# A message-passing kernel: how messages are added into their destination nodes, and how TensorE gets its addresses

## The chip, the cores and the metric

The kernel runs on one core of one Trainium2 chip. The metric is the device time of one execution in microseconds (us). The engines are PE (TensorE; PEld is its weight loads), DVE (VectorE), ACT (ScalarE), POOL (GpSimd) and SP (which here only issues transfers). Each has an in-order sequencer that decodes its instructions, computes registers and loads them, and hands the work to the engine proper; rows of a sequencer carry a q behind the engine's name (PEldq, POOLq).

## The reference

A graph of 3125 nodes with 64 features and 100,000 edges, sorted by destination. First three rounds with the same weights:

```python
msg_in = concat([h[src], h[dst], edge_attr], axis=1)
msg = silu(msg_in @ W1e + b1e) @ W2e + b2e
agg = segment_sum(msg, dst) / max(deg, 1)
h = h + silu(concat([h, agg]) @ W1n + b1n) @ W2n + b2n
```

After a residual and a layer norm, three relational layers: per relation the mean of `h[src]` over the edges of that relation into a node, times that relation's weight, plus a root term. A residual and a norm end it. All data is float32.

## The kernel before

Nodes stand in 25 blocks of 128 (`NB`), sources in 13 spans of two blocks (`NS`). A setup stage (to about 1522 us) ranks the edges and scatters their records (edge term, source place, destination place, type) into tiles of 128 edges whose sources lie in one span and whose destinations in one block. Eight tiles (`GT`) are a group, all with one destination block; there are `NG` = 160 groups. Then come six loops over the 160 groups: `l` = 0 to 2 are the rounds of the first network ("round 0" to "round 2" below), `l` = 3 to 5 the relational layers.

In a round, one group `g` runs through this:

- TensorE gathers. `gather_tile` (L871, L872, L875) multiplies three transposed one-hots of the tile (`ohT`: source in the span's first block, in its second, destination) by a table of node terms split in three bf16 parts, 192 columns wide. The table's column comes from registers, since the span and the block differ from tile to tile and from group to group. 24 matmuls fill four PSUM banks (`gat`); a half is two banks, and DVE must have read the half (`gat_read`) before the next group writes it.
- DVE adds the three parts and the record's edge term into `z`: three tensor_tensor for each half (L1274, L1277, L1280).
- ACT takes Silu into `msg` (L655), in float32.
- The scatter needs a one-hot of the destination places, `oh`, in float32. POOL compares four tiles of it (L523); ACT makes the other four with an Abs (L648) and a Relu (L652).
- TensorE, two groups later, adds `oh` times `msg` into PSUM (L897): 8 float32 matmuls of 64 columns (68 in round 0, which counts types), at a PSUM column from a register. PSUM holds the sums of all blocks for the whole round.

Addresses: `next_places` runs behind the first sums matmul. It loads 8 registers from `offsets` (L848), 1 from `goff` for the gather's destination (L850) and 1 from `goff` for the sums (L855). In round 0 DVE also makes `ohT` of each group from two broadcast rows (L1259, L1260), SP stores it, and rounds 1 to 5 load it again (L456); each group's record is loaded too (L442). In the relational layers sums are made per group in PSUM, ACT copies them (L670), and POOL adds them in three steps (L544, L547, L550) into an array in SBUF.

The order on each engine is written out by hand: a loop over four groups at a time, whose body says which group's step comes when.

## Time and profile before

| what | us |
|---|---|
| runs before (3) | 6181.42, 6185.32, 6193.58 (median 6185.32) |
| profiled execution | 6186.73 |
| its span | 6184.7 |
| setup | 0 to about 1522 |
| round 0, with its tail | 1522 to 2380 |
| round 1, round 2 | 2423 to 3200, 3245 to 4020 |
| relational layers | about 4070 to 6112 |

| engine | busy us | share |
|---|---|---|
| PE | 4992.0 | 81% |
| DVE | 3707.7 | 60% |
| POOL | 3328.4 | 54% |
| ACT | 2689.5 | 43% |

The span is the stretch from the first to the last recorded instruction. PE rows are modelled matmuls that overlap, so their length is not the distance from one to the next; that distance is seen in the chain of work that ended last. A granted clock of 1.00 is 2.4 GHz, 0.50 is 1.2 GHz.

### The profile page before, as it was taken

The numbers are of one execution on the slowest core, as the hardware profiler recorded it, in microseconds if no ns is written. First come the engines' busy times: TensorE is split into PE (matmuls) and PEld (weight loads), VectorE is DVE, ScalarE is ACT, GpSimd is POOL, SyncE is SP. The second block draws the span as 40 slices with busy tenths as digits, with TensorE's granted clock in tenths as the row PEclk, the third lists the DMA queues.
The fourth block names the chain that finished last, engine by engine and source line by source line (L and its number), as shares of the span: only waits on it lengthen the run. The fifth ranks groups of instructions, "written<-read, shape, count | busy, mean of one in ns | idle before, by whom it ended". The sixth has DMA issues, their size and how long they took to land.

```text
span 6184.7 us, 171993 instructions
## 1 busy us (share of the span) xinstructions
PE 4992.0 (81%) x47650; PEld 4584.0 (74%) x47651; DVE 3707.7 (60%) x9362; ACT 2689.5 (43%) x4966; POOL 3328.4 (54%) x4176
## 2 busy tenths in 40 slices
PE   3666666631888888888888888889999999999998
PEld 2444444421777776888878888879998999989997
DVE  6444444421777775555545555478885888768885
ACT  1111111112556565555545555555553555545553
POOL 1777777740555553444434444446663666636663
PEclk9999965555899998999989999999997999989997
DMA  8111111148899995666646666624442444324441
GB/s 311 29 29 29 29 29 29 29 117 260 282 291 305 301 305 188 220 221 220 221 153 224 221 222 221 201 92 132 132 132 72 133 133 132 128 79 133 132 132 58
DMA packets 358208, 975.40 MB, mean 158 GB/s; under 512 B 70911, under 2 KB 83539, under 8 KB 358154
## 3 DMA queue, kind: packets, MB, share of 16 engines
q1 hardware_dynamic: 317096, 946.00, 46.4%
q0 software_dynamic: 38400, 28.13, 2.6%
q10 hardware_dynamic: 2658, 0.51, 0.0%
q8 instruction: 38, 0.62, 0.0%
q14 instruction: 16, 0.13, 0.0%
HBM read 774.54 MB, written 199.05 MB: 157 GB/s over the span
## 4 chain that ended last, share of the span: by engine, by line
PE 67%; POOL 14%; issue 11%; DMA 4%; another core or an unknown queue 2%; DVE 2%; ACT 0%; POOLq 0%; SPq 0%; ACTq 0%; DVEq 0%
PE sums L902 20%; PE sums L897 15%; POOL recs L510 13%; PE gat L871 11%; PE gat L872 11%; PE gat L875 6%; DMA arena<-recs 2%; DMA recs<-arena 2%; PE gat L994 1%; PE gat L992 1%; PE sums L1005 1%; DVE arena L1149 0%; PE gat L794 0%; PE gat L976 0%
## 5 line engine op out<-in xcount | busy, mean ns | idle before, releaser
L523 POOL TENSOR_SCALAR arena<-iota_f,arena 128x128 f32<-128x128 f32 x1920 | 1210.5, 647 | 1471.1 <-PE sums L897 1285.2
L871 PE MATMUL gat<-table,arena 128*128 x7680 | 1945.3, 254 | 28.6 <-issue 12.8
L872 PE MATMUL gat<-table,arena 128*128 x7680 | 1945.5, 254 | 0.0
L902 PE MATMUL sums<-arena 128*128 128x192 bf16 x15360 | 1887.1, 246 | 0.0
L1293 DVE TENSOR_SCALAR arena<-iota_s,meta_t 128x512 bf16<-128x512 int16 x3840 | 1525.5, 470 | 360.6 <-PE sums L902 360.6
L897 PE MATMUL sums<-arena 128*128 128x64 f32 (+1 forms) x7680 | 1020.3, 278 | 414.1 <-issue 410.4
L902 PEld LDWEIGHTS sums<-arena 128*128 128x128 bf16 x15360 | 1325.2, 98 | 0.1
L897 PEld LDWEIGHTS sums<-arena 128*128 128x128 f32 x7680 | 946.4, 195 | 460.9 <-issue 459.9
L510 POOL DMA_INDIRECT recs<-arena x800 | 952.4, 1190 | 377.1 <-issue 372.2
L662 ACT CAST arena<-gat 128x768 bf16<-128x768 f32 x960 | 767.1, 799 | 808.5 <-PE gat L872 808.5
L648 ACT ACTIVATE arena<-iota_f,arena 128x128 f32<-128x128 f32 x1920 | 613.5, 390 | 953.7 <-PE sums L897 952.8
L875 PE MATMUL gat<-table,arena 128*128 x3840 | 997.0, 260 | 0.0
L1274 DVE TENSOR_TENSOR arena<-gat,arena 128x256 f32<-128x256 f32 x960 | 402.1, 419 | 730.5 <-PE gat L875 729.8
L871 PEld LDWEIGHTS gat<-table,arena 128*128 128x128 bf16 x7680 | 801.2, 104 | 40.3 <-issue 35.8
L872 PEld LDWEIGHTS gat<-table,arena 128*128 128x128 bf16 x7680 | 775.2, 101 | 7.1 <-issue 0.3
L544 POOL TENSOR_TENSOR arena<-arena 128x256 f32<-128x256 f32 x480 | 416.1, 867 | 652.1 <-ACT arena L670 651.3
L762 PE MATMUL gat<-arena 25*125 25x39 bf16 x800 | 232.1, 290 | 407.0 <-DVE arena L1120 407.0
L762 PEld LDWEIGHTS gat<-arena 25*125 25x125 bf16 x800 | 141.2, 176 | 450.1 <-DVE arena L1120 434.1
L608 ACT COPY arena<-gat 25x1000 bf16<-25x1000 bf16 x100 | 98.5, 985 | 835.2 <-PE gat L736 812.9
L550 POOL TENSOR_TENSOR arena<-arena 128x256 f32 x480 | 382.3, 796 | 94.8 <-POOL arena L547 94.8
L1277 DVE TENSOR_TENSOR arena<-arena,gat 128x256 f32<-128x256 f32 x960 | 404.0, 421 | 32.9
L1280 DVE TENSOR_TENSOR arena<-arena,gat 128x256 f32<-128x256 f32 x960 | 403.6, 420 | 32.8
(184 smaller groups left out, 4760.6 us busy)
## 6 DMA issues: line engine op xcount, KB each, us to landing
arena<-hots_d SPq DMA_DIRECT2D x320, 768.0 KB, 5.2
arena<-hots_d SPq DMA_DIRECT2D x480, 512.0 KB, 3.4
arena<-recs SPq DMA_DIRECT2D x640, 272.0 KB, 3.0
hots_d<-arena SPq DMA_DIRECT2D x160, 768.0 KB, 7.2
arena<-rows_d SPq DMA_DIRECT2D x160, 512.0 KB, 6.4
recs<-arena SPq DMA_DIRECT2D x1, 43520.0 KB, 119.2
recs<-arena POOLq DMA_INDIRECT x800, 2.9
arena<-in_edge_attr_dram SPq DMA_DIRECT2D x100, 62.5 KB
```

The source lines that it names most:

```text
L510: pool.indirect_dma_start(recs, bass.IndirectOffsetOnAxis(ap=addr_out[s][:, j:j + 1].bitcast(U32), axis=0), rec_out[s][:, j, :], None).the ...
L523: ins = pool.tensor_scalar(oh[u % 2][:, j, :], iota_f[:], rec_in[u][:, j, PLACE:PLACE + 1], None, ALU.is_equal)
L544: pool.tensor_tensor(part[:, :, 0:HID], part[:, :, 0:HID], part[:, :, HID:2 * HID], ALU.add).then_inc(part_step, 1)
L648: ins = act.activation(apart[:, j - POOL_HOTS, :], iota_f[:], ACT.Abs, bias=rec_in[u][:, j, PLACE:PLACE + 1], scale=-1.0)
L662: act.copy(gb[u % 4][:, 4 * h:4 * h + 4, :], gat[:, 1024 * h:1024 * h + 1024].rearrange("p (j w) -> p j w", j=4) [:, :, 0:K3]).then_inc(ga ...
L871: pe.matmul(at, ohT[u][:, 0, tile], table_flat[:, bass.ds(off[j], K3)], start=True, stop=False)
L872: ins = pe.matmul(at, ohT[u][:, 1, tile], table_next[:, bass.ds(off[j], K3)], start=False, stop=l >= LAYERS)
L875: ins = pe.matmul(at, ohT[u][:, 2, tile], table_flat[:, bass.ds(dst_off, K3)], start=False, stop=True)
L897: ins = pe.matmul(sums[:, bass.ds(to, w)], oh[s][:, j, :], msg[s][:, j, 0:w], start=False, stop=True, skip_group_check=True)
L902: ins = pe.matmul(accp[s][:, 256 * r:256 * r + K3], oh4[u][:, t, r * P:(r + 1) * P], gb[u][:, t, :], start=t == 0, stop=t == GT - 1)
L1277: dve.tensor_tensor(z[s][:, tiles, :], z[s][:, tiles, :], parts[:, tiles, HID:2 * HID], ALU.add).then_inc(z_step, 1)
L1293: ins = dve.tensor_scalar(oh4[u][:, j, :], iota_s[:], meta_t[:, bass.ds(GT * g + j, 1), PT - HID], None, ALU.is_equal)
```

## The change

The scatter of the three rounds is rebuilt.

- The message is split in three bf16 parts that add up to it, side by side in `parts`: ACT takes Silu twice, into float32 and into bf16 (the high part); what is left is subtracted by POOL in round 0 and by DVE in rounds 1 and 2 (between the two halves of the next group); ACT casts that to the middle part; POOL subtracts again for the low part.
- The one-hots are no longer compared on POOL and ACT. TensorE turns the group's destination `ohT` with 8 bf16 transposes into PSUM, and ACT copies the 8 x 128 columns to `oh`, in bf16. `ohT` stays in use until then, so its reload waits for `turned`.
- TensorE sums group g - 3 (`LAG`) with 8 bf16 matmuls of 192 columns (196 in round 0) into a per-group accumulator at a fixed place. ACT copies the accumulator, POOL adds the three parts (two adds of 64 columns) and adds the result into `macc` in SBUF (64 columns; in round 0 also 4 columns of counts). The means are taken from `macc`.
- Addresses lie in one table, `places`, with 11 numbers a group. TensorE loads 9 of them with one load, behind the group's sums; POOL loads one. The table gets its offsets over a transfer to DRAM and back.
- The relational layers keep their steps; only the table that their addresses come from is another.

Core of the diff (helpers, semaphores and buffers left out):

```diff
@@ -437,8 +441,6 @@
-                sp.wait_ge(oh_made, done(n - 4))
-                sp.wait_ge(apart_used, done(n - 4))
...
@@ -451,7 +453,10 @@
-                sp.wait_ge(gathered, done(2 * (l * NG + k - 4) + 1))
+                if l < LAYERS:
+                    sp.wait_ge(turned, done(l * NG + k - 4))
...
@@ -512,18 +519,59 @@
+                def low_part(g, u, l=l):
+                    n = l * NG + g
+                    s = u % 2
+                    if l == 0:
+                        pool.wait_ge(msg_ready, done(n))
+                        pool.wait_ge(low_made, done(n - 2))
+                        pool.sem_inc(acc_go, 1)
+                        pool.tensor_tensor(left[s], msg[s], parts[u][:, :, 0:HID], ALU.subtract).then_inc(left_made, 1)
+                    pool.wait_ge(mid_made, done(n))
+                    pool.sem_inc(acc_go, 1)
+                    pool.tensor_tensor(parts[u][:, :, 2 * HID:K3], left[s], parts[u][:, :, HID:2 * HID], ALU.subtract
+                                       ).then_inc(low_made, 1)
...
+                    reg = pool.alloc_register(f"macc_at{l}_{u}_{isinstance(g, int)}")
+                    pool.load([reg], places[0:1, bass.ds(ROW * g + GT + 1, 1)])
+                    to = pool.snap(reg, min_val=0, max_val=REC * (NB - 1))
+                    pool.wait_ge(acc_read, done(n))
+                    pool.wait_ge(added, done(n - 1))
+                    pool.sem_inc(acc_go, 1)
+                    pool.tensor_tensor(part[:, 0:HID], part[:, 0:HID], part[:, HID:2 * HID], ALU.add
+                                       ).then_inc(part_step, 1)
+                    pool.wait_ge(part_step, 2 * n + 1)
+                    pool.tensor_tensor(part[:, 0:HID], part[:, 0:HID], part[:, 2 * HID:K3], ALU.add
+                                       ).then_inc(part_step, 1)
+                    if l == 0:
+                        at = macc[:, bass.ds(to + HID, R)]
+                        pool.tensor_tensor(at, at, part[:, K3:W3], ALU.add)
+                    pool.wait_ge(part_step, 2 * n + 2)
+                    at = macc[:, bass.ds(to, HID)]
+                    pool.tensor_tensor(at, at, part[:, 0:HID], ALU.add).then_inc(added, 1)
...
-                        for j in range(POOL_HOTS):
-                            ins = pool.tensor_scalar(oh[u % 2][:, j, :], iota_f[:], rec_in[u][:, j, PLACE:PLACE + 1],
-                                                     None, ALU.is_equal)
-                        ins.then_inc(oh_made, 1)
...
+                        low_part(4 * i + u - 1, (u + 3) % 4)
+                        add_sums(4 * i + u - 4, u, i)
...
@@ -638,21 +686,32 @@
-                def messages(g, u, i, l=l):
+                def keep_hots(g, u, l=l):
                     n = l * NG + g
-                    act.wait_ge(rec_loaded[u], 16 * (QUADS * l + 1) + 16 * i)
-                    act.wait_ge(summed, done(n - 2))
-                    act.wait_ge(apart_used, done(n - 1))
-                    for j in range(POOL_HOTS, GT):
-                        ins = act.activation(apart[:, j - POOL_HOTS, :], iota_f[:], ACT.Abs,
-                                             bias=rec_in[u][:, j, PLACE:PLACE + 1], scale=-1.0)
-                    ins.then_inc(apart_made, 1)
-                    act.wait_ge(apart_made, n + 1)
-                    act.activation(oh[u % 2][:, POOL_HOTS:GT, :], apart, ACT.Relu, bias=ones[:, 0:1],
-                                   scale=-1.0).then_inc(apart_used, 1)
+                    act.wait_ge(summed, done(n - 4))
+                    act.wait_ge(turned, done(n))
+                    act.copy(oh[u], oh_ps[u % 2].rearrange("p (j n) -> p j n", n=P)).then_inc(hot_out, 1)
+                def messages(g, u, l=l):
+                    n = l * NG + g
+                    s = u % 2
+                    act.wait_ge(left_made, done(n - 2))
+                    act.wait_ge(summed, done(n - 4))
                     act.wait_ge(gat_read, done(2 * n + 1))
-                    act.activation(msg[u % 2][:, :, 0:HID], z[u % 2], ACT.Silu).then_inc(msg_ready, 1)
+                    act.activation(msg[s], z[s], ACT.Silu)
+                    act.activation(parts[u][:, :, 0:HID], z[s], ACT.Silu).then_inc(msg_ready, 1)
+                def middle(g, u, l=l):
+                    n = l * NG + g
+                    act.wait_ge(left_made, done(n))
+                    act.copy(parts[u][:, :, HID:2 * HID], left[u % 2]).then_inc(mid_made, 1)
+                def keep_msums(g, u, l=l):
+                    n = l * NG + g
+                    w = W3 if l == 0 else K3
+                    act.wait_ge(added, done(n - 2))
+                    act.wait_ge(summed, done(n))
+                    act.copy(msum[u % 2][:, 0:w], accp[u % 2][:, 0:w]).then_inc(acc_read, 1)
...
+                            keep_hots(4 * i + u, u)
+                            middle(4 * i + u - 1, (u + 3) % 4)
+                            keep_msums(4 * i + u - 4, u)
+                            messages(4 * i + u, u)
...
@@ -843,16 +910,12 @@
-                    pe.load(tile_regs[u % 2], offsets[0:1, bass.ds(GT * g, GT)])
+                def load_places(g, u, l=l):
                     if l < LAYERS:
-                        pe.load([dst_reg[u % 2]], goff[0:1, bass.ds(3 * g, 1)])
-                def load_sums(g, u, l=l):
-                    if l < LAYERS:
-                        pe.load([sum_reg[u % 2]], goff[0:1, bass.ds(3 * g + 1, 1)])
+                        pe.load(tile_regs[u % 2] + [dst_reg[u % 2]], places[0:1, bass.ds(ROW * g, GT + 1)])
...
@@ -877,80 +940,83 @@
+                def turn_dst_hots(g, u, l=l):
+                    n = l * NG + g
+                    pe.wait_ge(hot_out, done(n - 2))
+                    for j in range(GT):
+                        ins = pe.transpose(oh_ps[u % 2][:, j * P:(j + 1) * P], ohT[u][:, 2, j * P:(j + 1) * P],
+                                           ident_b[:])
+                    ins.then_inc(turned, 1)
...
                 def sums_ready(g, u, l=l):
                     n = l * NG + g
-                    pe.wait_ge(oh_made, done(n))
+                    pe.wait_ge(acc_read, done(n - 2))
                     if l < LAYERS:
-                        pe.wait_ge(apart_used, done(n))
-                        pe.wait_ge(msg_ready, done(n))
+                        pe.wait_ge(hot_out, done(n))
+                        pe.wait_ge(low_made, done(n))
                         if l == 0:
...
+                def sum_messages(g, u, l=l):
+                    w = W3 if l == 0 else K3
+                    sums_ready(g, u)
+                    for j in range(GT):
+                        ins = pe.matmul(accp[u % 2][:, 0:w], oh[u][:, j, :], parts[u][:, j, 0:w],
+                                        start=j == 0, stop=j == GT - 1)
+                    ins.then_inc(summed, 1)
...
-                        ins = pe.matmul(sums[:, bass.ds(to, w)], oh[s][:, j, :], msg[s][:, j, 0:w],
-                                        start=False, stop=True, skip_group_check=True)
...
+                            turn_dst_hots(g, u)
+                        if not known or g >= LAG:
+                            sum_messages(g - LAG, (u + 4 - LAG) % 4)
+                        if gathers:
+                            load_places(g + 1, u + 1)
...
@@ -1267,24 +1323,32 @@
+                        if l > 0 and h == 1 and (not isinstance(g, int) or g > 0):
+                            what_is_left(g - 1, (u + 3) % 4)
...
+                def what_is_left(g, u, l=l):
+                    n = l * NG + g
+                    dve.wait_ge(low_made, done(n - 2))
+                    dve.wait_ge(msg_ready, done(n))
+                    dve.tensor_tensor(left[u % 2], msg[u % 2], parts[u][:, :, 0:HID], ALU.subtract
+                                      ).then_inc(left_made, 1)
...
@@ -1308,33 +1372,28 @@
-                    dve.wait_ge(summed, done(l * NG + NG - 1))
+                    dve.wait_ge(added, done(l * NG + NG - 1))
```

On TensorE, in the loop of round 1, from the last gather matmul of a group to the end of its stage. Before:

```order
L875 MATMUL gat<-table,arena 128x192
L882 REGISTER_ALU
L897 ISA [waits msg_ready,apart_used,oh_made]
L897 MATMUL sums<-arena 128x64
L848 ISA
L848 TENSOR_LOAD offsets
L850 ISA
L850 TENSOR_LOAD goff
L855 ISA
L855 TENSOR_LOAD goff
L897 MATMUL sums<-arena 128x64 x7
L913 ISA
```

In the changed kernel:

```order
L938 MATMUL gat<-table,arena 128x192
L946 REGISTER_ALU
L948 MATMUL sums<-ident_b,arena 128x128 [waits hot_out]
L948 MATMUL sums<-ident_b,arena 128x128 x7
L968 MATMUL sums<-arena 128x192 [waits low_made,hot_out,acc_read]
L968 MATMUL sums<-arena 128x192 x7
L916 ISA
L916 TENSOR_LOAD places
L988 ISA
```

Three loads between the first and the second sums matmul became one behind the last, the sums lost their register step, and 8 transposes (`L948`) with a wait for `hot_out` came in.

On POOL, in round 0. Before, one group's share and the start of the next:

```order
L520 ISA [waits rec_loaded0]
L523 TENSOR_SCALAR arena<-iota_f,arena 128x128 [waits summed]
L523 TENSOR_SCALAR arena<-iota_f,arena 128x128 x3
L520 REGISTER_ALU [waits rec_loaded1]
L523 TENSOR_SCALAR arena<-iota_f,arena 128x128 [waits summed]
```

In the changed kernel, one group's share:

```order
L537 TENSOR_TENSOR arena<-arena 128x512 [waits low_made]
L540 TENSOR_TENSOR arena<-arena 128x8x64 [waits mid_made]
L547 ISA
L547 TENSOR_LOAD places
L548 ISA
L550 REGISTER_ALU [waits acc_read]
L552 TENSOR_TENSOR arena<-arena 128x64 [waits added]
L554 ISA
L555 TENSOR_TENSOR arena<-arena 128x64 [waits part_step]
L559 ISA
L559 TENSOR_TENSOR arena<-arena 128x4
L560 REGISTER_ALU
```

Four compares became two subtractions of 512 columns with ACT's cast between them (`mid_made`), and a chain of small adds behind them.

## Rows read from the trace of the kernel before

**Rows 1.** Windows of the three rounds: length, busy us and count per engine, clock, DMA.
```profile
1522.00:2380.00 858.00, 691.61 (x6352) 669.92 (x6352) 640.29 (x1591) 501.86 (x1027) 456.25 (x633) 0.91 0.90 294
2423.00:3200.00 777.00, 651.13 (x6396) 631.08 (x6394) 391.94 (x960) 401.29 (x955) 372.44 (x636) 0.97 0.66 219
3245.00:4020.00 775.00, 645.21 (x6395) 625.33 (x6392) 393.42 (x964) 401.89 (x956) 370.11 (x632) 0.97 0.65 217
```

**Rows 2.** TensorE's sequencer, round 1: ns min/median/max, first and last start (us).
```profile
L871 PEldq FUSED_REGOPS  x8: 37/37/42, 2802.2 to 2804.2; - x8
...
L848 PEldq TENSOR_LOAD <-offsets x1: 595/595/595, 2804.8 to 2804.8; - x1
...
L850 PEldq FUSED_REGOPS  x1: 51/51/51, 2805.5 to 2805.5; - x1
...
L855 PEldq FUSED_REGOPS  x1: 46/46/46, 2806.0 to 2806.0; - x1
L855 PEldq TENSOR_LOAD <-goff x1: 303/303/303, 2806.1 to 2806.1; - x1
...
L871 PEldq FUSED_REGOPS  x8: 37/37/42, 2807.4 to 2809.3; - x8
```

**Rows 3.** The same register loads over rounds 1 and 0, and layer 3.
```profile
L848 PEldq TENSOR_LOAD <-offsets x157: 587/595/612, 2433.0 to 3186.6; - x157
...
L848 PEldq TENSOR_LOAD <-offsets x123: 589/867/1727, 1720.8 to 2364.9; - x123
...
L848 PEldq TENSOR_LOAD <-offsets x153: 587/591/595, 4091.6 to 4693.5; - x153
```

**Rows 4.** Chain of work that ended last, round 1: start us, us, what.
```profile
2801.27 0.08 PE gat L875
2801.35 0.20 PE sums L897 x2
2801.55 0.21 issue
2801.76 1.75 PE sums L897 x14
```

**Rows 5.** Timeline, setup: start us, us, engine, line, tiles, count; transposes at L736.
```profile
406.63 1.02 PE L736 MATMUL gat<-ident_b,arena 125*25 125x125 bf16 x8
```

**Rows 6.** DVE by line: busy us, mean ns, then idle before; and one line's row.
```profile
L1277 DVE TENSOR_TENSOR arena<-arena,gat 128x256 f32<-128x256 f32 x320 | 134.6, 421 | 10.9
...
L1149 DVE TENSOR_TENSOR arena<-sums,b1e_all x100: 690/692/693, 93.0 to 1309.7; 125x512 f32<-125x512 f32 x100
```

**Rows 7.** ACT by line: busy us, mean ns, then idle before it with its releasers.
```profile
L655 ACT ACTIVATE arena<-arena 128x512 f32<-128x512 f32 x480 | 295.1, 615 | 14.8 <-DVE arena L1280 14.4
L608 ACT COPY arena<-gat 25x1000 bf16<-25x1000 bf16 x100 | 98.5, 985 | 835.2 <-PE gat L736 812.9 <-issue 22.3
...
L610 ACT COPY arena<-sums 128x125 f32<-128x125 f32 x100 | 26.5, 265 | 277.3 <-PE sums L757 277.3
...
L599 ACT CAST table<-nodes 128x512 bf16<-128x512 f32 x18 | 11.2, 620 | 0.8 <-DVE nodes L1196 0.4
```

**Rows 8.** POOL: an add of the relational layers (ns min/median/max), and by line.
```profile
L544 POOL TENSOR_TENSOR arena<-arena x480: 722/894/899, 4076.6 to 6109.9; 128x256 f32<-128x256 f32 x160
...
L1379 POOL MEMSET const-float32-1.0<- 128x1 f32 x1 | 0.1, 99 | 0.0
```

**Rows 9.** Transfers, 1720 to 2380 us (round 0): GB/s in 40 slices, and the sum.
```profile
GB/s 293 289 292 295 287 314 303 305 302 303 292 297 298 310 312 295 313 294 292 310 296 325 306 297 295 293 311 312 317 294 298 299 306 305 300 314 303 295 311 139
DMA packets 68770, 196.56 MB, mean 298 GB/s; under 512 B 5916, under 2 KB 5916, under 8 KB 68770
```

**Rows 10.** Round 0 at a low clock: the window's row, and two matmuls of its timeline.
```profile
2083.00:2087.60 4.60, 4.44 (x30) 4.33 (x31) 3.26 (x9) 2.23 (x5) 2.14 (x3) 0.65 0.92 277
...
2085.53 0.37 PE L871 MATMUL gat<-table,arena 128*128 x1
2085.69 0.37 PE L872 MATMUL gat<-table,arena 128*128 x1
```

243 lines of the change are left out of this document (117 added, 126 removed).

## Prediction

> **What bounds the kernel now.** I read the windows of the three rounds first, since the change rebuilds only these. No engine is full there: in round 1 PE is busy 651 of 777 us, DVE 392, ACT 401, POOL 372 [rows 1]. So the next view is the chain of work that ended last. In round 1 it stays on PE, but with "issue" in it, behind the first two passes of the sums [rows 4]: PE waited for nothing but its own sequencer. The third view is therefore the sequencer's own rows. It steps from one gather's registers to the next without a stop (8 tiles between 2802.2 and 2804.2), then come three register loads at 2804.8, 2805.6 (behind its step at 2805.5) and 2806.1, and the next group's first gather step follows at 2807.4 [rows 2]. This group crosses the loop's end; the mean distance of the offsets loads over round 1 is (3186.6 - 2433.0) / 156 = 4.83 us [rows 3]. PE's own work is 24 gather matmuls at 0.082 us (0.08 in the rows) = 1.97 and the sums 0.20 + 1.75 = 1.95 [rows 4], together 3.92. The sequencer sets the pace of rounds 1 and 2, and PE waits about 0.9 us a group for it.
>
> Round 0 has (2364.8 - 1720.6) / 122 = 5.28 us a group. The same loads stand in it, the first at a median of 0.87 us instead of 0.60 [rows 3]. Transfers are near a ceiling of their own: 196.56 MB for 123 groups is 1.60 MB a group, and the best slice moved 325 GB/s [rows 9], which makes 4.9 us.
>
> In the relational layers the distance is (4693.5 - 4091.6) / 152 = 3.96 us [rows 3], and PE's 48 matmuls of 192 columns at 0.082 us are 3.94. PE bounds them, the change leaves its work, and I cost them at nothing. The setup gets one more transfer (the table goes over DRAM). It stands on SP's queue beside POOL's scatters, which end the setup, so it costs nothing; uncovered it would be some 10 us at most. The drain of a round, behind its last gather, gets more links in its chain but sums of a third of the length (0.66 for 1.95 us a group). I take that as even, 5 us either way in each round.
>
> **Rounds 1 and 2, the sequencer.** Removed: two loads with their register steps, each the distance from 2805.5 to 2806.0, 0.48 us [rows 2], so 0.95. Removed too: the sums' register step, at the distance of the others: 8 tiles with 2 steps each and one more in 2.1 us, 0.12 [rows 2]. Added: a ninth register in the load, (0.595 - 0.303) / 7 = 0.04 [rows 2], and a wait for `hot_out` in front of the transposes, one step, 0.10. The matmuls themselves cost the sequencer next to nothing: gather steps with three matmuls between them come as closely as with two. Sum: 4.83 - 0.95 - 0.12 + 0.04 + 0.10 = 3.90 us.
>
> **PE's own work.** 24 x 0.082 for the gathers, 8 x 0.082 for sums of the same width and type, and 8 transposes of 128 columns. The setup's bf16 transposes of 125 columns took 1.02 us for 8, with one lasting 0.31, so 0.10 each [rows 5]; by columns from the gathers it is 0.055. Between 3.1 and 3.4 us, under the sequencer either way.
>
> **The other engines.** DVE: six adds at 0.42 with 0.03 between them, and `what_is_left` over 512 columns at the 0.69 of a 512-column add [rows 6]: 3.4. ACT: copy of 1024 columns 1.0 (1000 took 0.985), cast of 512 0.62, copy of 192 0.33 (between 0.265 for 125 and that), two Silu 1.23 [rows 7]: 3.2. POOL: 256 columns took 0.72 undisturbed, one column 0.10 [rows 8], so 2.4 ns a column: 512 columns 1.35, 64 columns 0.26. One subtraction and three adds are 2.1, with 0.4 for steps between, 2.5. The ends for POOL: a 512-column step costs no less than 256 columns (0.72) and no more than two at the disturbed 0.89 (1.79); a 64-column one between 0.10 and 0.72. At the upper ends a group is 1.79 + 3 x 0.72 + 0.4 = 4.4. The GPSIMD Engine Reference of the Trainium skill (3.1) gives 2.6 cycles an element for a two-input op, by which 512 columns would be an estimated 1.1 us; the slope of the rows here is a little steeper.
>
> **The new waits.** The engines now stand in a ring: DVE frees the half (`gat_read`), PE gathers it and turns the hots, ACT copies them, casts, copies sums and runs Silu, DVE subtracts and adds the second half two groups on. Half a gather 1.2, transposes 0.8, ACT 3.2, the subtraction 0.69, DVE's half 1.36: 7.25, and eight hand-overs at 0.05 to 0.13 (1.0 at most) make 7.6 to 8.3 for two groups, 3.8 to 4.15 each. That is level with 3.90. I take 4.0, and save (4.83 - 4.0) x 320 = 266 us in the two rounds.
>
> **Round 0.** The sequencer would come down by the same 0.93 to 4.35. But transfers stay at 4.9, and POOL gets a serial chain: subtraction, wait for ACT's cast, subtraction, then adds. (2 x 1.35 + 3 x 0.26 + 0.11 for 4 columns) = 3.6; DVE disturbs it by up to 0.894 / 0.722 = 1.24 [rows 8], I take 1.1 since its fast ops cover a third of the time: 3.95. Cast with hand-over 0.72, steps and hand-overs in between 0.6: 5.27 us, against 5.28 now. I save nothing there. Lower end: 4.9, the transfers. Upper end: 2 x 1.79 + 3 x 0.89 + 0.1 + 1.3 = 7.7. That four compares vanish from POOL and five activations and, in round 0, table loads from ACT costs or saves nothing: both engines waited for the sums.
>
> Sum: 6186.7 (profiled; 1.4 above the median of the runs) - 266 - 0 = 5920.
>
> **The rivals.**
> (a) Both soft terms come out at their good ends: round 0 at the transfers' 4.9, rounds 1 and 2 at 3.90. -61 - 298: **5828**.
> (b) The saved loads come back as waits. The sequencer halts at `gat_read`, so any lengthening of the ring is paid. With every ACT and DVE step of it a fifth longer the two groups take about 9, 4.5 each: -106, round 0 unchanged: **6081**. For it: ACT now writes strided bf16 of which no row has the price. Against it: ACT casts and bf16 copies fall on one line by columns [rows 7].
> (c) POOL bounds round 0 at 6.5, midway between 5.3 and 7.7: +195 - 266: **6116**. For it: mixed types and strided parts on POOL are in no row; at 7.7 it would be +387 and the kernel 2% slower.
> (d) The slower side: the clock. In round 0 there is a stretch at a clock of 0.65, and matmuls start 0.16 apart in it, where 0.08 is usual [rows 10]; round 0 has 0.91 on average and rounds 1 and 2 0.97 [rows 1]. At 1.2 GHz a group is 40 matmuls, at most 40 x 0.16 = 6.4 us of PE, more than anything else. If it held throughout, the rounds would cost +1.1 x 160 + 1.57 x 320 = +680: **6865**. The point at which it decides: 266 us over 480 groups is 0.55 a group, and a low group costs 1.1 to 2.4 more than in my sum, so a low share of about a quarter to a third eats the gain. Round 0 has 18% now (0.91). For it: PE idles in round 0 for 2 of 5.3 us, more than now (5.28 - 3.92 = 1.4). Against it: rounds 1 and 2 would be 80% busy as now, and at a low clock PE would be full.
> The Trainium skill (TensorE: Matmul & The Clock Gate, Part 4: PE-mode transpose) says that a transpose doesn't count as PE-busy for the clock. By that rule a fifth of the group's matmuls would be lost to it and (d) gains weight; no row of the rounds before has a transpose in it.
>
> **How the numbers follow.** Forecast 0.50, (a) 0.13, (b) 0.15, (c) 0.13, (d) 0.09. The forecast's own range, round 0 from 4.9 to 5.8 and the others from 3.9 to 4.15, is 5830 to 6050. The range given, 5820 to 6140, takes in (a), (b) and (c) and leaves out (d) and the far ends. A difference of 0.2% is about what a measurement of this kernel can tell from none. Faster: forecast, (a), (b), 0.06 of (c): 0.84. Same: 0.03 of (c). Slower: (d) and 0.04 of (c): 0.13.
>
> **What would show it.** TensorE's sequencer has one load a group, 3.9 to 4.1 us apart in rounds 1 and 2, with no stretch in front of the sums. A wait in front of `sum_messages` for `acc_read` or `low_made` in round 0 means POOL bounds it; DVE waiting for the rows means the transfers do. The relational layers last 2040 us as now. I am wrong if the loads keep their distance of 4.8, if the gather steps stand still at `gat_read`, or if the clock in the rounds falls under 0.85.

## The result, and the profile after

The changed kernel takes 6852.56 us (median of 4 runs, 6850.32 to 6856.48) beside 6184.76 for the kernel before on the same chip: a ratio of 1.1078, 95% interval 1.1059 to 1.1097. The forecast was 5920 with a range up to 6140. The kernel got slower instead of faster, and the forecast was off by 933 us.

The windows of the changed kernel, in the order round 0, round 1, round 2, first relational layer (length, busy us and count of PE, PEld, DVE, ACT, POOL, then clock, DMA share, GB/s):

```profile
1530.00:2590.00 1060.00, 706.69 (x6336) 611.62 (x6336) 699.02 (x1574) 447.35 (x794) 533.28 (x951) 0.82 0.73 239
2635.00:3457.00 822.00, 611.49 (x6384) 504.63 (x6381) 489.49 (x1119) 453.98 (x799) 318.64 (x632) 0.94 0.60 207
3505.00:4324.00 819.00, 608.83 (x6378) 499.41 (x6376) 488.69 (x1118) 453.60 (x799) 318.68 (x632) 0.95 0.59 205
4390.00:5133.00 743.00, 653.51 (x7612) 623.31 (x7610) 499.28 (x1248) 364.05 (x475) 380.49 (x478) 1.00 0.34 112
```

Against [rows 1] every round is longer, and no engine has become full: in round 1 PE is busy 611 of 822 us. The last row is the surprise. A relational layer took about 639 us before and takes 743 now, although the change leaves its matmuls, adds and compares alone, and the clock there is 1.00.

What the change does touch there is where the addresses come from. TensorE's sequencer in the changed kernel, over nearly whole stages: first L916 (9 registers, rounds 0 and 1), then L918 (8 registers, relational layer); ns min/median/max, first and last start.

```profile
L916 PEldq TENSOR_LOAD <-places x148: 850/2759/4531, 1599.8 to 2580.2; - x148
```
```profile
L916 PEldq TENSOR_LOAD <-places x160: 842/2167/2193, 2634.4 to 3449.3; - x160
```
```profile
L918 PEldq TENSOR_LOAD <-places x157: 592/1935/1957, 4391.3 to 5122.9; - x157
```

The rows to set beside these are [rows 3]: eight registers at a median of 0.595 us in round 1, 0.87 in round 0, 0.591 in the relational layers. Now nine take 2.17 and the same eight take 1.94. The minimum is 0.85 and 0.59, though, so some loads are fast. Four consecutive groups of round 1 show which, in two answers:

```profile
L916 PEldq TENSOR_LOAD <-places x3: 2164/2167/2171, 3003.5 to 3014.1; - x3
```
```profile
L916 PEldq TENSOR_LOAD <-places x1: 852/852/852, 3019.3 to 3019.3; - x1
```

Three slow, one fast. A row of `places` has 11 words, so the first word of group g is word 11g of the table, and that is a multiple of four for every fourth group. In `before` a group starts at word 8g of `offsets`, always a multiple of four.

What the slow load does is seen in the chain of work that ended last, round 1 of the changed kernel (start us, us, what):

```profile
3004.49 0.43 DVE arena L1341
...
3004.95 0.43 DVE arena L1341
3005.38 0.76 issue
3006.14 0.25 PE gat L934
3006.39 0.12 PE gat L935
```

The load began at 3003.5 and ended at 3005.7. DVE has finished what it can by 3005.38, nothing is awaited, and the first gather of the next group comes at 3006.14, behind the sequencer. In round 1 "issue" holds 17.4% of the chain (three lines of DVE hold 37%, so that the chain alone could also speak for the ring of waits), and over the whole span the row of waits (engine, line, releaser: us, times, longest) is

```profile
PEld gat L934 <- issue: 1264.4, 837, 12.4
```

The account, in distances from load to load, with the means over a stage (161 loads; for round 0 that is its whole length, ramp included, which is why it shows 5.42 and not the 5.28 of the prediction):

| stage | before | after | groups | difference |
|---|---|---|---|---|
| round 0 | 5.42 | 6.73 | 160 | +208 us |
| rounds 1 and 2 | 4.81, 4.79 | 5.12, 5.10 | 320 | +97 |
| relational layers | 3.93 | 4.67 | 480 | +353 |
| sum | | | | +658 |

The spans differ by 6848.6 - 6184.7 = 664. Over half of the loss lies in the layers that the prediction costed at nothing, and in rounds 1 and 2 a saving was turned into a loss.

The engines' own steps came near the forecast, POOL's apart. Groups of the changed kernel's page and lines (busy us, mean ns, idle before):

```profile
L540 POOL TENSOR_TENSOR arena<-arena 128x512 bf16<-128x512 f32 x480 | 532.4, 1109 | 1487.4 <-ACT arena L707 1487.1
...
L562 POOL TENSOR_TENSOR arena<-arena 128x64 f32 x480 | 153.9, 321 | 68.5 <-POOL arena L555 63.8
```
```profile
L693 ACT COPY arena<-sums 128x1024 bf16<-128x1024 bf16 x480 | 485.9, 1012 | 1350.1 <-PE sums L948 1350.1
...
L707 ACT CAST arena<-arena 128x512 bf16<-128x512 f32 x480 | 298.5, 622 | 17.7 <-POOL arena L537 15.8 <-DVE arena L1350 1.7
...
L714 ACT COPY arena<-sums 128x192 f32<-128x192 f32 (+1 forms) x480 | 155.1, 324 | 9.5 <-POOL arena L562 9.5
```
```profile
L1350 DVE TENSOR_TENSOR arena<-arena 128x512 f32<-128x512 f32 x320 | 219.6, 686 | 2.6 <-ACT arena L702 2.6
```

The sum had 0.69 for DVE's subtraction (0.686), 1.0, 0.62 and 0.33 for ACT (1.012, 0.622, 0.324), and for POOL 1.35 and 0.26 (1.109 and 0.32). POOL's 512 columns were too dear in the sum by 0.24 us, its 64 columns too cheap by 0.06. The 2.6 cycles an element of the Trainium skill (GPSIMD Engine Reference, 3.1), an estimated 1.1 us for 512 columns, are nearer to the measured 1.109 than the slope from [rows 8] is.

### The profile page after: what moved, and what is told of

The parts are those of the page before. It is cut to its first block, busy times and chain, and to the rows that moved or that the text cites. A ratio compares the mean times of both kernels' runs of the same rounds, so it can differ in the third digit from the quotient of the medians.

```text
span 6848.6 us, 173813 instructions
## 1 busy us (share of the span) xinstructions
PE 5012.6 (73%) x47638; PEld 4266.5 (62%) x47639; DVE 3956.2 (58%) x9658; ACT 2734.1 (40%) x4407; POOL 3299.2 (48%) x4499
## 4 chain that ended last, share of the span: by engine, by line
PE 47%; DVE 16%; issue 13%; POOL 13%; ACT 5%; DMA 3%; another core or an unknown queue 2%; DVEq 1%; POOLq 0%; SPq 0%; ACTq 0%
PE sums L977 17%; POOL recs L517 12%; PE gat L934 11%; PE gat L935 10%; DVE arena L1341 6%; ACT arena L721 4%; PE gat L938 4%; DVE arena L1337 4%; DMA arena<-recs 2%; DVE arena L1350 2%; PE sums L968 1%; DVE arena L1316 1%; DMA recs<-arena 1%; PE sums L948 1%
## 5 line engine op out<-in xcount | busy, mean ns | idle before, releaser
L934 PE MATMUL gat<-table,arena 128*128 x7680 | 1997.7, 260 | 1073.8 <-DVE arena L1341 356.3
L935 PE MATMUL gat<-table,arena 128*128 x7680 | 2005.3, 261 | 0.0
L934 PEld LDWEIGHTS gat<-table,arena 128*128 128x128 bf16 x7680 | 779.9, 102 | 1323.5 <-issue 1264.4
L540 POOL TENSOR_TENSOR arena<-arena 128x512 bf16<-128x512 f32 x480 | 532.4, 1109 | 1487.4 <-ACT arena L707 1487.1
L938 PE MATMUL gat<-table,arena 128*128 x3840 | 1046.8, 273 | 0.0
L693 ACT COPY arena<-sums 128x1024 bf16<-128x1024 bf16 x480 | 485.9, 1012 | 1350.1 <-PE sums L948 1350.1
L935 PEld LDWEIGHTS gat<-table,arena 128*128 128x128 bf16 x7680 | 780.6, 102 | 132.2 <-issue 0.3
L968 PE MATMUL sums<-arena 128*128 128x192 bf16 (+1 forms) x3840 | 439.4, 261 | 10.6 <-ACT arena L714 10.6
L938 PEld LDWEIGHTS gat<-table,arena 128*128 128x128 bf16 x3840 | 414.6, 108 | 18.7 <-issue 0.2
L729 ACT COPY arena<-sums 128x768 f32<-128x768 f32 x480 | 386.7, 806 | 9.9 <-PE sums L977 9.9
```

The lines of the kernel that those rows point to most:

```text
L540: pool.tensor_tensor(parts[u][:, :, 2 * HID:K3], left[s], parts[u][:, :, HID:2 * HID], ALU.subtract).then_inc(low_made, 1)
L693: act.copy(oh[u], oh_ps[u % 2].rearrange("p (j n) -> p j n", n=P)).then_inc(hot_out, 1)
L934: pe.matmul(at, ohT[u][:, 0, tile], table_flat[:, bass.ds(off[j], K3)], start=True, stop=False)
L935: ins = pe.matmul(at, ohT[u][:, 1, tile], table_next[:, bass.ds(off[j], K3)], start=False, stop=l >= LAYERS)
L938: ins = pe.matmul(at, ohT[u][:, 2, tile], table_flat[:, bass.ds(dst_off, K3)], start=False, stop=True)
L968: ins = pe.matmul(accp[u % 2][:, 0:w], oh[u][:, j, :], parts[u][:, j, 0:w], start=j == 0, stop=j == GT - 1)
```

## Experiments

Three theories stood against each other. **A**: a register load that starts off a multiple of four words reads each word by itself. **B**: the new table, its place or the longer load is slow as such, or the new ring of waits. **C**: the load is slow because of where it stands now (behind the sums, beside other traffic). Of the first four runs two are the changed kernel with only the row's length altered, one is the kernel before with its table moved, one is the kernel before with the single load. The run with rows of 12 words is called the aligned kernel from here on.

### Rows of 12 words instead of 11

```diff
-    ROW = GT + 3
+    ROW = 12
...
-            sp.dma_start(places_v[0:1, 0:NG, GT:ROW], goff_i[0:GP, :, :]).then_inc(tables_in, 16)
+            sp.dma_start(places_v[0:1, 0:NG, GT:GT + 3], goff_i[0:GP, :, :]).then_inc(tables_in, 16)
```

> The changed kernel with one number altered: a row of the address table is 12 words long instead of 11 (the twelfth is unused), so that every row starts on a multiple of 4 words. Theory A (a register load is slow when its first word isn't on a multiple of 4 words): every load of 9 registers takes 0.85 us instead of 2.17 in three of four groups; the relational layers return to 3.95 us a group (-350 us), rounds 1 and 2 come to 4.1 to 4.3 us a group, round 0 to about 5.3; in all 5940 to 6020 us. Theory B (the loads are slow because the table is larger or written in short pieces, or the ring of waits through the three-part scatter sets the pace): no change, 6850 us. Theory C (the place of the load behind the sums costs it): loads 0.85 us, but the groups of rounds 1 and 2 stay near 5.1.

**5861.59 us** (5857.19 to 5864.63), ratio to before 0.9473 (0.9458 to 0.9489). One unused word in a row turns 10.8% slower into 5.3% faster. That is theory A's direction, and 78 us below the range expected for it: round 0 took 4.90 where about 5.3 was expected, rounds 1 and 2 4.02 where 4.1 to 4.3 was. The same three stages of this kernel, sequencer's loads:

```profile
L916 PEldq TENSOR_LOAD <-places x145: 846/1385/2345, 1599.1 to 2290.9; - x145
```
```profile
L916 PEldq TENSOR_LOAD <-places x159: 836/846/869, 2352.2 to 2988.4; - x159
```
```profile
L918 PEldq TENSOR_LOAD <-places x161: 587/592/605, 3742.0 to 4371.6; - x161
```

and its windows of round 0, round 1 and the first relational layer:

```profile
1530.00:2300.00 770.00, 577.85 (x6336) 472.33 (x6336) 667.84 (x1579) 470.00 (x796) 569.68 (x949) 0.98 0.96 330
2350.00:2996.00 646.00, 569.24 (x6374) 460.10 (x6371) 490.93 (x1117) 456.13 (x799) 365.78 (x632) 1.00 0.79 264
...
3742.00:4380.00 638.00, 635.92 (x7678) 634.32 (x7679) 508.11 (x1280) 367.39 (x479) 379.75 (x476) 1.00 0.42 132
```

The slow loads are gone. Rounds 1 and 2 have (2988.4 - 2344.4) / 160 = 4.02 us a group, the relational layers 3.935 as before, round 0 4.90. From changed to aligned: (6.73 - 4.90) x 160 + (1.10 + 1.08) x 160 + 0.737 x 480 = 293 + 349 + 354 = 996, where the spans differ by 6848.6 - 5858.9 = 990. So the whole loss, and more, is the row's length; B and C fall as causes of it.

### Rows of 14 words

Set beside the aligned kernel:

```diff
-    ROW = 12
+    ROW = 14
```

> The changed kernel with rows of 14 words: every second row starts on a multiple of 4 words, the others on a multiple of 2. Theory A: half of the loads are fast, the relational layers' loads average (0.60 + 1.94) / 2 = 1.27 us and the distance of groups is about 4.4 us; in all near 6500 us. If an even word is enough, all are fast and the time is that of rows of 12 words. Theory B: 6850 us.

**6548.09 us**, ratio 1.0583 (1.0562 to 1.0604). Now every second group starts on a multiple of four. Relational layer:

```profile
L918 PEldq TENSOR_LOAD <-places x161: 587/604/1972, 4194.3 to 4903.8; - x161
```

The loads alternate between 0.60 and 1.96 (mean 1.27), a group takes 4.43. An even word isn't enough. The loss against the aligned kernel is 0.50 us a group here and 0.74 with rows of 11 words, close to the ratio of the slow loads, a half to three quarters. So it is set by the start of the row, not by its length.

### The kernel before, its table one word later

```diff
-            sp.dma_start(offsets[0:1, 0:NT], off_i[:]).then_inc(tables_in, 16)
+            sp.dma_start(offsets[0:1, 1:NT + 1], off_i[:]).then_inc(tables_in, 16)
...
-                    pe.load(tile_regs[u % 2], offsets[0:1, bass.ds(GT * g, GT)])
+                    pe.load(tile_regs[u % 2], offsets[0:1, bass.ds(GT * g + 1, GT)])
```

> The kernel before with its table of offsets moved by one word (and read one word later), nothing else. Theory A: each load of 8 registers takes 1.94 us instead of 0.60, in all six loops; a group of the relational layers 4.9 us instead of 3.96, of rounds 1 and 2 about 6.2 instead of 4.83, round 0 more than 6.6: 7200 to 7500 us. Theory B: nothing changes, 6185 us.

**7519.49 us**, ratio 1.2153 (1.2129 to 1.2177). Nothing of the change is in this kernel. Its loads of round 1:

```profile
L848 PEldq TENSOR_LOAD <-offsets x161: 1937/1942/1947, 2661.8 to 3716.9; - x161
```

All 161 take 1.94 us, with hardly any spread. The cost follows the word at which the load starts and needs neither the table `places` nor the load's new position. The relational layers go to 5.00 us a group, +1.06 for 1.35 more in the load: PE's queued matmuls hide the rest. Round 1 goes the other way, from 4.81 to (3716.9 - 2661.8) / 160 = 6.59, +1.78 a group for 1.35. Here 6.2 was expected, and the total lies just above the 7200 to 7500 expected. The window of round 1 has a clock of 0.78:

```profile
2661.00:3720.00 1059.00, 838.71 (x6359) 804.81 (x6360) 396.85 (x960) 400.84 (x955) 366.09 (x628) 0.78 0.50 160
```

PE stood idle in each group, and the granted clock is lower than the 0.97 of [rows 1]. What that costs can be read from the chain of work that ended last. By line, over round 1, first the kernel before and then this one, with one stretch of this one's sums:

```profile
by line: PE sums L897 40.0%; issue 16.1%; PE gat L872 14.6%; PE gat L871 14.6%; PE gat L875 14.6%; DVE arena L1280 0.1%
```
```profile
by line: PE sums L897 37.6%; issue 20.8%; PE gat L871 13.9%; PE gat L872 13.8%; PE gat L875 13.7%; DVE arena L1277 0.1%; DVE arena L1274 0.1%; DVE arena L1280 0.0%; DVEq L1276 0.0%
...
2767.98 3.22 PE sums L897 x14
```

Times the distance of a group, "issue" goes from 0.77 to 1.37 us, +0.60, and PE's own steps from 4.03 to 5.21, +1.17, with the same matmuls in them: 14 passes of the sums took 3.22 us at 2767.98 where [rows 4] has 1.75. So in the rounds PE's queue hides 0.75 of the load's 1.35, and the slower matmuls at the lower clock cost 1.17 on top. That PE's idle time is what brought the clock down isn't tested: no run here holds one and changes the other.

### The kernel before with one load a group

One table of 12-word rows and one load of 10 registers in the rounds, where `before` has three loads; the scatter of before stays (8 float32 matmuls into PSUM, one-hots compared on POOL and ACT).

```diff
-                    pe.load(tile_regs[u % 2], offsets[0:1, bass.ds(GT * g, GT)])
...
-                        pe.load([dst_reg[u % 2]], goff[0:1, bass.ds(3 * g, 1)])
+                        pe.load(tile_regs[u % 2] + [dst_reg[u % 2], sum_reg[u % 2]],
+                                places[0:1, bass.ds(ROW * g, GT + 2)])
```

> The kernel before with one part of the change alone: all addresses in one table with rows of 12 words, and in the rounds one load of 10 registers instead of three loads (the place of the sums is stored two rows later, so that one row has all that a stage needs). The scatter is the old one. If the load was what rounds 1 and 2 waited for: it takes about 1.1 us instead of 1.7 with its steps, a group 4.4 instead of 4.83 us, and the whole 6000 to 6060 us. If the new scatter is what brings the gain of the aligned change, this stays within 0.5% of 6185.

**5995.36 us**, ratio 0.9693 (0.9677 to 0.971). The load in round 1:

```profile
L859 PEldq TENSOR_LOAD <-places x161: 1072/1078/1103, 2388.2 to 3077.5; - x161
```

Ten registers take 1.08 us, nine 0.85, eight 0.595: 0.24 for each of the two behind the eighth. A group takes 4.31, which closes the prediction's account with one term altered: 4.81 - 0.95 (two loads with their steps) + 2 x 0.24 = 4.34. Two loads less were worth what the sum said; a ninth register costs 0.24 and not 0.04. The total came 5 us under the 6000 to 6060 expected. The aligned kernel is another 5995 - 5862 = 133 us faster, 0.29 us a group in rounds 1 and 2. Not all of that is the new scatter's own (bf16 parts, turned one-hots, sums in SBUF): this kernel's tenth register costs 0.23, and its sums still have their register step. The new scatter needs neither, since its accumulator stands at a fixed place; what it is worth beyond that isn't separated here.

### Two loads again in the aligned kernel

```diff
-                        pe.load(tile_regs[u % 2] + [dst_reg[u % 2]], places[0:1, bass.ds(ROW * g, GT + 1)])
+                        pe.load(tile_regs[u % 2], places[0:1, bass.ds(ROW * g, GT)])
+                        pe.load([dst_reg[u % 2]], places[0:1, bass.ds(ROW * g + GT, 1)])
```

> The aligned kernel (rows of 12 words), with the nine-register load of a group in the rounds split into one of eight registers and one of a single register. This puts back one of the two loads a group that the change took out, and nothing else. The prediction's sum had the second load at 0.30 us and the ninth register at 0.04. In the aligned kernel the nine-register load takes 0.845 us and a group of rounds 1 and 2 is 4.02. If the sequencer still sets the pace there: 0.595 + 0.30 = 0.90 us instead of 0.845 and one more issue, so 4.05 to 4.15 a group, +0.05 to +0.1 us over 314 groups, total 5875 to 5905 us: merging the two loads was worth a fifth of what the two loads cost, since the ninth register costs 0.25 and not 0.04. If it is the number of loads that costs (each with its own fixed part of about 0.3 us, as the prediction took it): 4.28 a group, 5940 us. The relational layers stay at 3.935 either way.

**5935.57 us** (5932.39 to 5937.01), ratio to before 0.9583 (0.9567 to 0.9599), +74 on the aligned kernel. Groups of rounds 1 and 2 take 4.24, and the two loads of round 1 are

```profile
L916 PEldq TENSOR_LOAD <-places x161: 587/592/612, 2353.1 to 3031.1; - x161
```
```profile
L917 PEldq TENSOR_LOAD <-places x161: 303/308/322, 2353.7 to 3031.9; - x161
```

I expected 5875 to 5905 and was wrong. What came is what the same expectation gave for the case that each load costs by itself, 4.28 a group and 5940. The loads themselves grow by only 0.592 + 0.308 - 0.846 = 0.05, but the distance by 0.21. A second load brings its register step and the gap to it, together 0.48 (the distance read in [rows 2]), less the 0.24 to 0.25 of the ninth register. The length of an instruction's row is not its price on a sequencer; the distance to the next one is.

### Twelve registers instead of nine

```diff
-                        pe.load(tile_regs[u % 2] + [dst_reg[u % 2]], places[0:1, bass.ds(ROW * g, GT + 1)])
+                        pe.load(tile_regs[u % 2] + [dst_reg[u % 2]] + spare_regs, places[0:1, bass.ds(ROW * g, ROW)])
```

> The aligned kernel, with the load of the rounds filling 12 registers instead of 9 (the three more are not used). Theory A: a load reads four words at a time where it starts on a multiple of four, and what is left over one word at a time, 0.24 us a read. Then 9 registers are 2 + 1 reads (0.845 us measured) and 12 are 3 reads: the load stays at 0.83 to 0.86 us, and the time within 0.2% of 5862. Rival B: each register costs by itself, 0.24 us for each after the eighth (8: 0.595, 9: 0.845, 10: 1.08): 12 registers take 1.55 us, a group of rounds 1 and 2 takes 4.7, and the total is 6080 us or more.

**5863.64 us** (5859.77 to 5870.49), ratio to before 0.9473 (0.9457 to 0.9488), the aligned kernel's own.

```profile
L917 PEldq TENSOR_LOAD <-places x161: 844/849/869, 2344.5 to 2988.4; - x161
```

Twelve registers cost what nine do. So each register does not cost by itself. The picture that fits all lengths measured is this: from a multiple of four the load takes four words in a step of about 0.24 us. A tenth register costs another 0.23 where only ten are loaded (1.08), yet twelve cost 0.85: a full four is one step, and what is left over at the end goes singly. Off the multiple, 8 words are 8 steps and 9 words 9: 1.94 and 2.17.

### Half of round 0's index rows

The destinations' row isn't sent and their one-hots are made from the row of the sources, so 256 KB a group less are transferred and the messages of round 0 go to the wrong places. All engine instructions stay.

```diff
-                sp.dma_start(row_in[u % 2], rows_by_group[:, bass.ds(k, 1), :].rearrange("m a e -> a m e")
-                             .to_broadcast([P, 2, GT * P])).then_inc(rows_loaded[u % 2], 16)
+                sp.dma_start(row_in[u % 2][:, 0:1, :], rows_by_group[0:1, bass.ds(k, 1), :].rearrange("m a e -> a m e")
+                             .to_broadcast([P, 1, GT * P])).then_inc(rows_loaded[u % 2], 16)
...
-                    dve.tensor_scalar(to[:, 2, :], row_in[u % 2][:, 1, :], lane[:, 0:1], None, ALU.is_equal
+                    dve.tensor_scalar(to[:, 2, :], row_in[u % 2][:, 0, :], lane[:, 0:1], None, ALU.is_equal
```

> The aligned kernel, with half of round 0's index rows left out: one of the two 1024-word rows of a group is broadcast (256 KB instead of 512 KB), and the one-hots of the destinations are made from the row of the sources, so that the messages of round 0 go to wrong places; every engine instruction stays. In the aligned kernel a group of round 0 takes 4.90 us with the DMA engines busy 0.96 of the time at 330 GB/s. Theory T (the transfers bound round 0): 16% fewer bytes, so 4.1 to 4.4 us a group until the next bound, total 5735 to 5800 us. Theory P (GpSimd's chain of 5.27 us a group, as the prediction had it, or TensorE with its loads) binds: a group stays at 4.8 to 4.9, total 5850 to 5870. Rounds 1 and 2 and the relational layers stay at 4.02 and 3.935.

**5844.53 us** (5841.61 to 5849.17), ratio to before 0.9441 (0.9425 to 0.9456). The whole is 17 us less than the aligned kernel's, and a group of round 0 goes from 4.90 to (2270.9 - 1506.7) / 160 = 4.78, below the 4.8 to 4.9 of theory P and far above the 4.1 to 4.4 of theory T. Between 1720 and 2200 us, though, nothing is gained; the 20 us of round 0 lie before and behind. The same load in that stretch, in the aligned kernel and here:

```profile
L916 PEldq TENSOR_LOAD <-places x102: 846/1300/2163, 1721.4 to 2199.8; - x102
```
```profile
L916 PEldq TENSOR_LOAD <-places x101: 850/1114/1382, 1721.8 to 2195.3; - x101
```

That is 478.4 / 101 = 4.74 us and 473.5 / 100 = 4.74 us a group. The chain over round 0 names what ended last, here for the aligned kernel:

```profile
by line: DMA arena<-rows_d 66.5%; issue 10.2%; DVE arena L1315 6.5%; DVE arena L1316 5.9%; DVE arena L1341 3.5%; DVE arena L1337 2.5%; DVE arena L1329 1.3%; SPq L435 0.6%; DVEq L1336 0.6%; DVEq L1328 0.5%; DVEq L1340 0.4%; DVEq L1311 0.2%; 
```

and here with half the rows:

```profile
by line: POOL arena L537 23.1%; issue 18.9%; POOL arena L540 17.6%; ACT arena L707 13.3%; POOLq L547 7.7%; POOL arena L552 7.2%; POOL arena L559 2.6%; POOL arena L555 2.5%; POOL arena L562 1.7%; POOLq L559 1.0%; POOLq L554 0.9%; POOLq L551 
```

In the aligned kernel the transfers end last. With a sixth of them taken away it is the serial chain on POOL: subtraction, ACT's cast, subtraction, the adds, and in between POOL's own register load (L547). But that load is not the same in the two kernels. Over round 0, with half the rows and in the aligned kernel:

```profile
L547 POOLq TENSOR_LOAD <-places x160: 288/1112/1369, 1542.0 to 2282.9; - x160
```
```profile
L547 POOLq TENSOR_LOAD <-places x160: 284/294/1617, 1546.0 to 2302.1; - x160
```

The means are 1.07 and 0.46 us, and 0.29 in rounds 1 and 2 of both. With half the rows 154 of the 160 loads overlap in time with one of DVE's one-hot compares (L1315, L1316) and take 1.10 on average, the other six 0.29. In the aligned kernel 47 overlap and take 0.79, the other 113 take 0.33. So this run took transfers away and made POOL's chain 0.6 us longer at once. It shows that a sixth fewer bytes hardly speed up the round as this kernel stands. It does not show how near POOL's chain lies to the transfers in the aligned kernel, and which of the two would bind without the other stays open.

### One load for two groups

Table rows of 24 words, 18 registers at every second group (16 in the relational layers).

```diff
+                    if u % 2:
+                        return
...
-                        pe.load(tile_regs[u % 2] + [dst_reg[u % 2]], places[0:1, bass.ds(ROW * g, GT + 1)])
+                        pe.load(tile_regs[0] + tile_regs[1] + dst_reg, places[0:1, bass.ds(ROW // 2 * g, 2 * GT + 2)])
```

> The aligned kernel, with one register load for two groups (table rows of 24 words, 18 registers in the rounds, 16 in the relational layers, at every second group). Theory A (four words a read where aligned, 0.24 us a read and 0.11 fixed): 18 registers are 4 + 2 reads, 1.55 us for two groups against 1.69 now, 0.07 us a group less: rounds 1 and 2 at 3.95, relational layers 16 registers 1.07 against 1.19, 0.06 a group less if the sequencer binds there; total 5830 to 5855 us. Rival B (a fixed part of 0.3 us a load, the rest by registers): 18 registers cost more than 3 us and a pair stalls TensorE: slower than 5862. Rival C: a long load in one piece stalls TensorE, whose matmuls of the group before have run out by then, where two short ones were covered: no gain although the sum of the loads falls, 5862 or more.

**5949.82 us** (5948.44 to 5953.43), ratio to before 0.961 (0.9594 to 0.9626): 88 us slower than the aligned kernel, though the loads behave as theory A has them (0.11 + 6 x 0.24 = 1.55 for 18 registers):

```profile
L918 PEldq TENSOR_LOAD <-places x81: 1585/1592/1611, 2356.6 to 3024.9; - x81
```
```profile
L920 PEldq TENSOR_LOAD <-places x81: 1102/1106/1126, 3802.0 to 4442.8; - x81
```

1.59 for two groups is less than 2 x 0.85, but a pair takes (3024.9 - 2356.6) / 80 = 8.35 us where it took 8.05. In the group without a load the sequencer stands still at its wait for `gat_read`. Rows of this kernel around that wait: the last step before it (in `gather_tile`, 32 ns) and the first behind it.

```profile
L933 PEldq ALU_OP  x1: 32/32/32, 2705.4 to 2705.4; - x1
```
```profile
L936 PEldq FUSED_REGOPS  x1: 37/37/37, 2706.1 to 2706.1; - x1
```

That is 0.6 us in which the sequencer waits for DVE in one group, and a full 1.6 us of load, begun 1.3 us later, in the next. PE's own idle time in front of a gather, four groups in a row (in brackets, us; the profile names DVE for each, but at 2709.97 the load of 2707.4 to 2709.0 and the sequencer's steps behind it ended last):

```profile
2701.45 0.25 PE L936 MATMUL gat<-table,arena 128*128 x1 [1.11 <-DVE arena L1343]
2706.15 0.25 PE L936 MATMUL gat<-table,arena 128*128 x1 [0.18 <-DVE arena L1343]
2709.97 0.25 PE L936 MATMUL gat<-table,arena 128*128 x1 [1.50 <-DVE arena L1343]
2714.69 0.25 PE L936 MATMUL gat<-table,arena 128*128 x1 [0.17 <-DVE arena L1343]
```

Behind the long load PE stands idle for 1.1 and 1.5 us, in the group without one for 0.2. What the short group gains it can't keep, since only two halves of `gat` let it run ahead. The rival C of the expectation (no gain, although the sum of the loads falls) is the one that came. A relational pair takes 8.01 instead of 7.87. There PE, which nothing stopped in the aligned kernel, now waits for its own sequencer behind some of the loads of 1.1 us; the waits of that layer (3810 to 4440 us) have this row, where the aligned kernel's have none of the kind:

```profile
PEld sums L979 <- issue: 7.4, 38, 0.3
```

That is 7.4 of the 11 us which the layer lost; the rest isn't placed.

## Why the prediction was wrong

**The step that failed** is "Added: a ninth register in the load, (0.595 - 0.303) / 7 = 0.04". It drew a line through a load of one word, which is one step at any start, and one of eight words from a multiple of four, which is two, and took the price of a load to be a matter of its number of registers. The load became 2.17 us in three groups of four and 0.85 in the fourth, mean 1.83. Two errors are in that step. The slope was wrong even for aligned loads (0.24 and not 0.04, since eight registers come in fours): 0.2 us on the sequencer's sum, of which the 4.0 taken had left room for a half. And the start of the row, at a multiple of 11 words, was in the diff but was not looked at, worth 990 us.

**The relational layers "at nothing"** failed through the same hole. "The change leaves its work" looked at PE's matmuls alone; the diff takes their eight registers from the new table as well, and 0.60 became 1.60 on average. With PE otherwise full, 0.74 of the 1.0 came through, 353 us.

**Round 0** was 6.73 over its whole length, where the kernel before had 5.42 and the forecast was no change. Its loads take 3.0 us on average and not the 1.83 of the quiet rounds. In the aligned kernel the load there is 1.41 and a group 4.90. The prediction's 5.28 and 4.9 are distances without the ramp, and beside them the aligned kernel has the 4.74 of 1720 to 2200 us, under the "transfers' 4.9" that was the lower end: the transfers reached 335 GB/s on average, above the 325 of the best slice. The forecast's POOL chain of 5.27 was over-sized. Its two subtractions were put at 1.35 x 1.1 each where 1.09 and 1.11 were measured, 0.8 us in all, and even with a register load of 1.07 in the chain, which the sum didn't have, a group took 4.74. So in the aligned kernel the likeliest value lost to the good end of rival (a) by the size of two terms, the subtractions and the transfers' rate. That transfers end last was allowed for as the lower end. That POOL's chain lies close behind them isn't shown.

**Rounds 1 and 2** were right as far as the sum concerns what the change was about. The aligned kernel has 4.02 us for 4.0, and with the ninth register at its real price the sequencer alone gives 3.90 - 0.04 + 0.25 = 4.11, 0.09 too much, so that 4.0 was met partly by luck. Nothing stops the sequencer there: the eight gather steps of a group follow each other in 2.0 us, at the pace of [rows 2], with the next load right behind the sums. TensorE's sequencer in the aligned kernel, one group of round 1:

```profile
L934 PEldq FUSED_REGOPS  x8: 37/37/42, 2704.2 to 2706.2; - x8
```

The "ring" of 3.8 to 4.15 didn't bind in it, and its size isn't shown by any run: the kernel with a load for two groups has a wait for `gat_read` at 4.18 a group, but its long load is part of that distance. Transposes came at 11.1% of the chain of round 1, 0.45 us for eight or 0.056 each, the lower end.

**The rivals.** (a) is nearest to the aligned kernel: 5828 against 5862. (b)'s stop at `gat_read` isn't in the aligned kernel, and (c) put round 0 at 6.5 for POOL's chain; where POOL's chain ended last, with half the rows, a group took 4.78. (d) named the right total (6865 for 6853) for a wrong reason, which is luck. The clock in round 0 did fall, from 0.91 to 0.82, but in rounds 1 and 2 it is 0.94 and 0.95, and the relational layers lose the most at 1.00. The aligned kernel issues the same matmuls and transposes at 0.98 in round 0 and 1.00 in round 1. So the low clock went with PE standing idle and not with what it ran (what a low clock costs is in the run with the shifted table); how much of the 0.25 us in round 0 that the load's growth leaves over (6.73 - 4.90 - 1.58) it took isn't settled. The rule of the Trainium skill that a transpose doesn't count as PE-busy (TensorE: Matmul & The Clock Gate, Part 4) cost nothing visible here: the clock is 1.00 in round 1 of the aligned kernel, with 8 transposes among 40 matmuls.

**"What would show it"** held as a test: the loads were 5.1 apart and not 3.9 to 4.1, the relational layers didn't keep their 2040 us. The clock of round 0 fell under 0.85 as well (0.82). It named these as signs of failure without a rival that could bring the 5.1 or the longer relational layers.

The version to keep is the aligned kernel: 5861.59 us, 0.9473 of before, with one spare word in a row.

## What to carry to other kernels

Where a diff moves the table that a sequencer loads its registers from, work out the first word of every load modulo four before anything else, and pad rows to a multiple of four words. Price an instruction on a sequencer by the distance to the next one, and look for each line whose operand changed, in stages too whose work is left alone. When the sequencer sets the pace, spread its long steps evenly; a sum that shrinks in fewer, longer pieces can cost more.

## What the runs showed of the hardware

- A register load on TensorE's sequencer in quiet stretches (rounds 1 and 2, relational layers): 0.30 us for 1 word at any start, 0.595 for 8, 0.85 for 9 or 12, 1.08 for 10, 1.11 for 16, 1.59 for 18, the longer ones when they start on a multiple of four words. Multiples of four that are none of eight do as well: rows of 12 words have them in every second group, and their nine registers took 0.836 to 0.869 in round 1. Off it: 1.94 for 8 words and 2.17 for 9, whether the start is 1, 2 or 3 words off (the shifted kernel has 1, the 14-word rows 2, the 11-word rows all three).
- In round 0 these loads are longer: the aligned nine took 1.41 on average, the changed kernel's 3.0 instead of 1.83. The rate of the transfers alone doesn't explain it. The aligned kernel moves 264 GB/s in round 1 with its loads unstretched (0.836 to 0.869), the changed one 239 GB/s in round 0.
- POOL's single word took 0.29 where it stood clear of DVE's one-hot compares with half the rows, and 1.10 where it overlapped one; in the aligned kernel 0.33 and 0.79. For TensorE's aligned nine the same split gives 1.25 and 1.52 (66 and 95 loads), so the compares are at most a part of it there. No run takes the compares away, and the cause stays open.
- At a granted clock of 0.61 (2766 to 2772 us of the shifted kernel) 14 passes of the float32 sums took 3.22 us, at 0.97 over the round in the kernel before 1.75.
- The aligned kernel's transfers reached 353 GB/s in a slice of round 0 (335 on average), above the 325 that the prediction took as the best slice of before [rows 9].
